# Batches 6 and 7 of a fused Mamba and mixture-of-experts kernel: two sums of the step size moved to VectorE, the gate products moved behind the scans of step 1

## The chip, the cores and the metric

The kernel runs on one core of one Trainium2 chip. The metric is the device time of one execution in microseconds (us); the number that counts is the median of several runs.

## The reference

The input `x` is 8 batches of 512 tokens with 128 features, float32. The result is `x + mamba(layernorm(x)) + moe(layernorm(x))`. What matters here is the Mamba block; per batch it computes:

```python
u = silu(causal_conv(xn @ in_proj))                   # 256 channels, 512 tokens
dt_raw, B, C = split(u @ x_proj)                      # 8, 16 and 16 columns
delta = softplus(dt_raw @ dt_proj.T + dt_proj_b)      # the step size
dA, dBu = exp(delta * A), delta * u * B               # for each of 16 states
h[t] = dA[t] * h[t-1] + dBu[t]                        # a scan along the tokens
y = sum over 16 states of h * C + u * D
y = y * silu(z)                                       # the gate
out = y @ out_proj + residual
```

The expert layer routes each token to 2 of 8 experts with 352 hidden units; its tiles of 128 tokens are worked off beside the scans of batches 1 to 5, and their results are gathered back in batches 5 to 7.

## The kernel before

The kernel is one program in which the order of the instructions of every engine is written out by hand; engines meet in counted semaphores, and each engine works through its own list in order. A wait that isn't met holds all that stands behind it on that engine.

The time is cut into 8 batches of 16 steps, one step for each state. Below, "step 6.3" is batch 6, state 3. The 256 channels lie as two halves of 128 partitions, so an ordinary operation is 128x512. In a step:

- ScalarE makes the decay factor `exp(delta * A)` of each half (`decay`, L502, into a buffer in SBUF; `decay_bank`, L514, into a bank of PSUM).
- The scan's input is either made by GpSimd (`scaled`, L915, in steps 6.0, 6.1, 6.2, 6.4, 7.0 and 7.1) or, in the other steps of batches 6 and 7 (the list `BY_PE`), by ScalarE in time-major form (`scaled`, L530, four instructions) and then transposed by TensorE into the scan's bank, one half at a time (`dbu_turn`, L1376).
- VectorE runs the scan of each half (`scan`, L1128), then multiplies each half with its row of C (`product`, L1145). In batches 6 and 7 both scans come before both products.
- TensorE transposes the products and adds them up over the states (`accumulate`, L1413). This happens in banks 2 and 3, a step later.

At the end of a batch ScalarE copies the sum out (`y_evac`, L681), TensorE turns it back to channel-major form in the same banks 2 and 3 (`y_turn`, L1506), and VectorE multiplies it with the gate (`gate`, L1153), which frees the banks for the next batch. So the first `accumulate` of a batch has a wait of its own:

```python
wait(pe, "p_rdy", 2 * (n + 1))
if k == 0:
    wait(pe, "g_rdy", 2 * b)
```

TensorE meets it in step 1. Behind it on TensorE stand, in step 6.1, `skip` (L1425), `rows(7)` (L1460) and a filler product `keep` (L1321); in step 6.2 the next `accumulate`, the first half of `dbu_turn` for step 6.3, a `skip` and a `keep`; and at the head of step 6.3 its second half. In step 7.1 the first half of `dbu_turn` for step 7.2 stands directly behind it, then a `keep`, then the second half.

Also at the start of batches 6 and 7 the scan's input in natural form is turned for ScalarE: TensorE writes it to banks 5 and 4 (`input_turn`, L1394), ScalarE copies it out (`input_turned`, L541). Bank 5 is the bank of the first scan of steps 6.1 and 7.1. In step 7.1 the scan waits for that copy itself:

```python
if b == NB - 1 and k == 1 and hf == 0:
    dve.wait_ge(s["dut_rdy"], 6)
```

The step size of the next batch is worked out beside the scans. In batch 6, for batch 7: ScalarE takes magnitudes (L740, L741) and `exp(-|v|)` (`vanishing`, L746) in steps 4 and 6, then in step 7 `rounded` (L751, `1 + y`, 128x1024) and `corrected` (L756, that minus 1), and the logarithm in step 10 (L761). GpSimd adds and corrects (`raise_sum`, L427; `correct`, L433) in steps 5 to 10. Right behind `corrected` ScalarE has the tanh of the z branch of batch 6 (`z_gate`, L664), VectorE follows with its product (L1244) at the end of step 6.8, and TensorE with the second z product (`z_mm`, L1498), which stands in front of the second half of `dbu_turn` for step 6.9.

GpSimd issues the indirect DMAs of the expert layer's gathers in these steps (L964).

Of the kernel before, what the change touches and what calls it, by code (L numbers as in the profile page):

```python
# [7 lines left out]
ALU = mybir.AluOpType  # L8
# [4 lines left out]
def build(nc, x, norm_w, w_in, conv_w, conv_b, x_proj, dt_proj, dt_b, a_log, d_par, w_out,  # L13
# [42 lines left out]
    with ctx:  # L56
        def sb(name, shape, dt=FP32):
            return ctx.enter_context(nc.sbuf_tensor(name, shape, dt))
# [81 lines left out]
        sp_y = sb("sp_y", [P, NH, T])  # L140
        sp_e = sb("sp_e", [P, NH, T])
        sp_d = sb("sp_d", [P, NH, T])
# [59 lines left out]
        s = {k: sem(k) for k in names}  # L202
# [57 lines left out]
        STEPS_AT = {b: (4, 6) if b == 6 else (2, 3) for b in range(NB - 1)}  # L260
        LOG_AT = {b: 10 if b == 6 else 8 for b in range(NB - 1)}
# [198 lines left out]
        def _(act):  # L460
# [179 lines left out]
            def late(b, k):  # L640

                if k in STEPS_AT[b]:
                    vanishing(b + 1, STEPS_AT[b].index(k))
                if k == STEPS_AT[b][1] + 1:
                    rounded(b + 1)
                if k == LOG_AT[b] - 3:
                    corrected(b + 1)
                if k == COLS_AT.get(b):
                    columns(b + 1)
# [356 lines left out]
        def _(dve):  # L1006
# [103 lines left out]
            def scan(b, k, hf):  # L1110

                n = b * S + k
                at = bank_of(b, 2 * k + hf)[:, :]
                dve.wait_ge(s["da_rdy"], 2 * n + hf + 1)
                if n in BY_PE:
                    dve.wait_ge(s["dbu_rdy"], 2 * turned_before(n) + hf + 1)
                    inp = at
                elif n == 0:
                    dve.wait_ge(s["dbu_0"], NH)
                    inp = dbu[0][:, hf, :]  # L1120
                else:
                    wait(dve, "dbu_p", 2 * pooled_before(n) + hf + 1)
                    inp = dbu[k % 2][:, hf, :]
                if b == NB - 1 and k == 1 and hf == 0:
                    dve.wait_ge(s["dut_rdy"], 6)
                elif b == NB - 1 and k == 1:
                    wait(dve, "p_rdy", 2 * S * b + 1)
                nc.vector.tensor_tensor_scan(at, da_of(n)[:, hf, :] if n in IN_SBUF else at, inp, 0.0,  # L1128
                                             ALU.mult, ALU.add).then_inc(s["h_rdy"], 1)
# [17 lines left out]
            def gate(b):  # L1147

                wait(dve, "o_mm", b)
                dve.wait_ge(s["yb_mm"], 2 * b + 2)  # L1150
                dve.wait_ge(s["z_rdy"], 2 * b + 2)
                for hf in range(NH):
                    nc.vector.tensor_tensor(g_sb[:, hf, :], zs_sb[:, hf, :], YB[hf][:, :], ALU.mult).then_inc(s["g_rdy"], 1)  # L1153
# [27 lines left out]
            def combine(b):  # L1181
# [4 lines left out]
                nc.vector.tensor_tensor(a_b, (GB, UB)[(b + 1) % 2][:, :].rearrange("p (t c) -> p t c", t=TT), a_b,  # L1186
                                        ALU.add).then_inc(s["comb"], 1)

            def step0(k):
                scan(0, k, 0)  # L1190
                scan(0, k, 1)
                product(0, k, 0)
                product(0, k, 1)
                if k in LATE_ROWS:
                    rows_normed(*LATE_ROWS[k])
                if k == 5:
                    st(nc.vector.reciprocal(irms[:, :], sxh))
                    st(nc.vector.tensor_tensor(irms[:, :], irms[:, :], rstd, ALU.mult))
                if k in (1, 4):
                    unit(1, k // 4)  # L1200
                if k == 7:
                    choices()
                if k in (11, 14):
                    unit(2, k // 14)
                if k in z_step(0):
                    z_gate(0, k)
                if k == 10:
                    weights()
                for g in HOT_STEP.get(k, ()):
                    one_hots(g)  # L1210

            def step(b, k):
                j = tile(b * S + k)
                scan(b, k, 0)
                if b >= 6:
                    scan(b, k, 1)
                if j is not None:
                    first_product(j)
                product(b, k, 0)
                if b < 6:  # L1220
                    scan(b, k, 1)
                if j is not None:
                    second_product(j)
                product(b, k, 1)
                if k == 0:
                    gate(b - 1)
                if b == 1 and k == 0:
                    sources()
                if b > 5 and k == PROJECT_AT[b] + 1:
                    store(b - 1, GB)  # L1230
                if b == 7 and k in z_step(b):
                    z_gate(b, k)
                elif b == 6 and k - 1 in z_step(b):
                    z_gate(b, k - 1)
                if k in (11, 14) and b + 2 < NB:
                    unit(b + 2, k // 14)
                if b * S + k in COMBINE_AT:
                    combine(COMBINE_AT[b * S + k])
# [62 lines left out]
            b = NB - 1  # L1301
# [480 lines left out]
```

## Time and profile before

| | |
|---|---|
| median of 3 runs | 633.02 us (633.02 to 634.33) |
| time of the profiled execution | 634.19 us |
| its span in the trace | 632.4 us |
| TensorE busy | 545.9 us (86%) |
| VectorE busy | 591.2 us (93%) |
| ScalarE busy | 457.4 us (72%) |
| GpSimd busy | 509.4 us (81%) |
| mean granted TensorE clock | 0.965 |

The profile gives one execution. PE is TensorE, DVE VectorE, ACT ScalarE, POOL GpSimd. The timeline view lists an engine's instructions in order of time, with like ones merged into one row (x2 for two); in square brackets stands how long the engine was idle before it, and what released it. The starts of the steps of batches 6 and 7 are read from the scans of VectorE: step 6.0 begins at 503.54 us, step 7.0 at 567.16 us.

### The profile page before, as it was taken

Reading aid. Unit: us, or ns where it says so; the run is one execution under the profiler, and the core shown is the slowest. Engines: PE = TensorE matmul, PEld = TensorE weight load, DVE = VectorE, ACT = ScalarE, POOL = GpSimd, SP = SyncE. Lnnn points to the kernel's source line nnn. Section 1 sums busy time; section 2 is a strip of 40 time slices with the busy share of each in tenths; the row PEclk is TensorE's granted clock in tenths of the full one; section 3 lists DMA queues with packets and bytes.
Section 4 is the critical chain, followed back from the end, with each engine's and each line's share of the span. In section 5 each row is a group of like instructions: output and inputs, shape, how many; then the busy total and the mean of one; then the engine's idle time right before and its main releaser. Section 6 shows DMA issues by size and latency. Waiting matters only on the chain.

```text
span 632.4 us, 11492 instructions
## 1 busy us (share of the span) xinstructions
PE 545.9 (86%) x3560; PEld 427.7 (68%) x3560; DVE 591.2 (93%) x852; ACT 457.4 (72%) x916; POOL 509.4 (81%) x481
## 2 busy tenths in 40 slices
PE   5969988888899998989899898998989697878887
PEld 2368765655877777777687677777777465656564
DVE  6967989999989998999989999899989999899997
ACT  1784899127877698667976688776986579969881
POOL 5795039638999989998999989999898978875783
PEclk9867979979999999999999999999999999899999
DMA  7320106834668788778878788678894345332473
GB/s 221 131 101 0 46 27 127 288 129 158 217 220 262 264 292 252 258 246 266 291 263 270 232 278 285 228 267 269 299 265 157 136 157 216 121 122 80 117 138 84
DMA packets 60894, 122.99 MB, mean 194 GB/s; under 512 B 8219, under 2 KB 41379, under 8 KB 53795
## 3 DMA queue, kind: packets, MB, share of 16 engines
q1 hardware_dynamic: 53826, 112.42, 52.3%
q0 software_dynamic: 6288, 9.52, 7.1%
q8 instruction: 29, 0.48, 0.3%
q10 hardware_dynamic: 720, 0.33, 0.3%
q14 instruction: 31, 0.25, 0.1%
HBM read 112.77 MB, written 9.47 MB: 193 GB/s over the span
## 4 chain that ended last, share of the span: by engine, by line
PE 43%; DVE 21%; ACT 18%; issue 15%; DMA 2%; POOL 0%; DVEq 0%; ACTq 0%
DVE bank L1128 8%; PE bank L1413 8%; PE bank L1562 7%; PE bank L1445 7%; DVE h_sb L1145 6%; PE bank L1576 5%; PE bank L1570 4%; ACT dbu L530 3%; ACT bank L514 2%; PE bank L1468 2%; ACT da L502 2%; PE bank L1460 2%; PE bank L1543 1%; PE bank L1376 1%; DVE lo_oh L1087 1%
## 5 line engine op out<-in xcount | busy, mean ns | idle before, releaser
L915 POOL TENSOR_TENSOR dbu<-du,xn_all 128x512 f32<-128x512 f32 x172 | 215.4, 1275 | 26.8 <-DVE bank L1128 26.4
L1128 DVE TENSOR_TENSOR_SCAN bank<-bank,dbu 128x512 f32<-128x512 f32 x170 | 207.2, 1221 | 9.0 <-ACT bank L514 8.9
L1145 DVE TENSOR_TENSOR h_sb<-bank,xh_all 128x512 f32<-128x512 f32 x240 | 159.3, 678 | 1.2
L514 ACT ACTIVATE bank<-delta,a_sb 128x512 f32<-128x512 f32 x170 | 116.8, 689 | 54.2 <-DVE h_sb L1145 53.5
L1413 PE MATMUL bank<-id_sb,h_sb 128*128 128x128 f32 x992 | 134.8, 281 | 15.2 <-DVE h_sb L1145 13.6
L1413 PEld LDWEIGHTS bank<-id_sb,h_sb 128*128 128x128 f32 x992 | 115.3, 145 | 26.8 <-DVE h_sb L1145 20.4
L1128 DVE TENSOR_TENSOR_SCAN bank<-da,bank 128x512 f32<-128x512 f32 x82 | 96.7, 1214 | 17.1 <-PE bank L1376 17.0
L1562 PEld LDWEIGHTS bank<-wd_sb,hid 117*128 117x128 f32 (+1 forms) x432 | 55.1, 190 | 57.8 <-DVE hid L1179 33.1
L1562 PE MATMUL bank<-wd_sb,hid 117*128 117x128 f32 (+1 forms) x432 | 63.7, 283 | 28.3 <-ACT xT L687 26.7
L902 POOL DMA_INDIRECT xs<-xn_rows,src x72 | 70.7, 981 | 12.4 <-issue 9.1
L530 ACT ACTIVATE dbu<-du_t,bc_sb 128x256 f32<-128x256 f32 x164 | 69.4, 496 | 4.5 <-DVE bank L1128 2.9
L1376 PE MATMUL bank<-id_sb,dbu 128*128 128x128 f32 x328 | 54.2, 291 | 18.2 <-ACT dbu L530 10.1
L1376 PEld LDWEIGHTS bank<-id_sb,dbu 128*128 128x128 f32 x328 | 39.8, 148 | 40.2 <-issue 22.2
L1445 PE MATMUL bank<-xhT,wk_sb 128*128 128x512 f32 x128 | 61.3, 607 | 0.7 <-ACT xhT L473 0.7
L502 ACT ACTIVATE da<-delta,a_sb 128x512 f32<-128x512 f32 x86 | 58.0, 713 | 4.7 <-DVE bank L1128 4.5
L1570 PE MATMUL bank<-xT,wgu_sb 128*118 128x128 f32 x432 | 59.2, 273 | 0.3 <-DVE ga L1172 0.2
L1576 PE MATMUL bank<-xT,wgu_sb 128*118 128x128 f32 x432 | 59.1, 272 | 0.0
L964 POOL DMA_INDIRECT xhT<-y_slots,slot x40 | 38.7, 966 | 18.5 <-DVE bank L1128 6.8
L1576 PEld LDWEIGHTS bank<-xT,wgu_sb 128*118 128x118 f32 x432 | 52.7, 181 | 0.5 <-issue 0.5
L1570 PEld LDWEIGHTS bank<-xT,wgu_sb 128*118 128x118 f32 x432 | 52.3, 182 | 0.7 <-issue 0.7
L705 ACT ACTIVATE ys<-bank,stat 128x128 f32<-128x128 f32 x72 | 26.3, 366 | 33.1 <-PE bank L1562 33.0
L698 ACT ACTIVATE th<-bank 118x384 f32<-118x384 f32 x72 | 34.8, 483 | 19.1 <-PE bank L1570 18.4
(197 smaller groups left out, 902.9 us busy)
## 6 DMA issues: line engine op xcount, KB each, us to landing
xh_all<-b_rows SPq DMA_DIRECT2D x30, 1024.0 KB, 7.2
xn_all<-b_rows SPq DMA_DIRECT2D x25, 1024.0 KB, 7.2
wgu_sb<-in_w_gu SPq DMA_DIRECT2D x72, 352.0 KB, 2.9
wd_sb<-in_w_dn SPq DMA_DIRECT2D x72, 192.0 KB, 3.3
y_slots<-ys SPq DMA_DIRECT2D x72, 64.0 KB
xn_rows<-xn_all SPq DMA_DIRECT2D x2, 1040.0 KB, 9.9
out<-x_sb SPq DMA_DIRECT2D x7, 256.0 KB, 6.8
x_sb<-in_x SPq DMA_DIRECT2D x2, 640.0 KB, 5.7
```

The lines of the kernel that those rows point to most:

```text
L514: nc.scalar.activation(bank_of(b, m)[:, :], delta[b % 2][:, hf, :], ACT.Exp, scale=a_sb[:, hf, k:k + 1]).then_inc(s["da_rdy"], 1)
L530: last = nc.scalar.activation(dbuT[k % 2][:, t, :], duT[:, t, :], ACT.Copy, scale=bc_sb[q][:, t, k:k + 1])
L902: nc.gpsimd.indirect_dma_start(xs[i][:, :], None, xn_rows, bass.IndirectOffsetOnAxis(ap=src[:, j:j + 1], axis=0)).then_inc(s[f"xs_in{i}"], 16)
L915: nc.gpsimd.tensor_tensor(dbu[k % 2][:, hf, :], du[b % 2][:, hf, :], b_ring[c % 2][:, k % CH, :], ALU.mult).then_inc(s["dbu_p"], 1)
L1128: nc.vector.tensor_tensor_scan(at, da_of(n)[:, hf, :] if n in IN_SBUF else at, inp, 0.0, ALU.mult, ALU.add).then_inc(s["h_rdy"], 1)
L1145: nc.vector.tensor_tensor(h_sb[k % 2][:, hf, :], bank_of(b, 2 * k + hf)[:, :], row, ALU.mult).then_inc(s["p_rdy"], 1)
L1376: last = nc.tensor.transpose(at[:, t * P:(t + 1) * P], dbuT[k % 2][:, t, hf * P:(hf + 1) * P], id_sb[:, :])
L1413: last = MM(HT[i][:, t % 2, hf * P:(hf + 1) * P], h_sb[k % 2][:, hf, t * P:(t + 1) * P], id_sb[:, :], is_transpose=True, start=(k == 0 and ...
L1445: last = MM(at[:, :], wk_sb[:, tap, hf * P:(hf + 1) * P], xhT[:, c, tap:tap + T], start=(tap == taps[0] if c == 0 else tap == 0), stop=(ta ...
L1562: last = MM(XD[:, P:P + H], hid[j % 2][0:FN[c], c * P:(c + 1) * P], wd_sb[j % NW][0:FN[c], c, :], start=(c == 0), stop=(c == NF - 1))
L1570: last = MM(GB[0:FW, c * P:(c + 1) * P], wgu_sb[j % NW][:, c * FS:c * FS + FW], xT[j % 2][:, :], start=True, stop=True)
L1576: last = MM(UB[0:FW, c * P:(c + 1) * P], wgu_sb[j % NW][:, F + c * FS:F + c * FS + FW], xT[j % 2][:, :], start=True, stop=True)
```

## The change

Two things. In batch 6 `rounded(7)` and `corrected(7)` leave ScalarE (both in step 6.7) and are done by VectorE as `tensor_scalar` instructions of 128x1024, the first at the end of step 6.7, the second at the end of step 6.8, each behind the step's products and ahead of the z product. In batches 6 and 7 the two gate products of the batch before leave the end of step 0; they now stand in step 1, behind both scans and ahead of both products. Batches 1 to 5 stay as they are. The waits of the other engines are unchanged.

```diff
@@ ScalarE, late(b, k)
-                if k == STEPS_AT[b][1] + 1:
+                if b < 6 and k == STEPS_AT[b][1] + 1:
                     rounded(b + 1)
-                if k == LOG_AT[b] - 3:
+                if b < 6 and k == LOG_AT[b] - 3:
                     corrected(b + 1)
@@ VectorE
+            def rounded(c):
+
+                dve.wait_ge(s["sp_exp"], 2 * c + 2)
+                nc.vector.tensor_scalar(sp_d[:, :, :], sp_y[:, :, :], 1.0, None, ALU.add).then_inc(s["sp_w"], 1)
+
+            def corrected(c):
+
+                dve.wait_ge(s["sp_w"], c)
+                nc.vector.tensor_scalar(sp_e[:, :, :], sp_d[:, :, :], -1.0, None, ALU.add).then_inc(s["sp_corr"], 1)
+
@@ VectorE, step(b, k)
                 scan(b, k, 0)
                 if b >= 6:
                     scan(b, k, 1)
+                if b >= 6 and k == 1:
+                    gate(b - 1)
                 if j is not None:
                     first_product(j)
                 product(b, k, 0)
@@ VectorE, step(b, k)
                 product(b, k, 1)
-                if k == 0:
+                if b < 6 and k == 0:
                     gate(b - 1)
+                if b == 6 and k == STEPS_AT[b][1] + 1:
+                    rounded(b + 1)
+                if b == 6 and k == STEPS_AT[b][1] + 2:
+                    corrected(b + 1)
```

## Rows read from the trace of the kernel before

**Rows 1.** The page, part 1: busy us, share of the span, instructions.

```profile
PE 545.9 (86%) x3560; PEld 427.7 (68%) x3560; DVE 591.2 (93%) x852; ACT 457.4 (72%) x916; POOL 509.4 (81%) x481
```

**Rows 2.** Windows view: stretch, its us, busy by engine, granted PE clock, DMA, GB/s.

```profile
519.40:529.60 10.20, 8.41 (x55) 6.28 (x54) 10.20 (x13) 10.20 (x22) 8.10 (x9) 1.00 0.64 246
575.80:625.00 49.20, 44.21 (x274) 31.36 (x272) 49.20 (x60) 38.04 (x79) 35.17 (x27) 1.00 0.50 113
...
568.00:570.00 2.00, 2.00 (x12) 2.00 (x11) 2.00 (x4) 2.00 (x5) 1.84 (x3) 0.52 0.97 401
```

**Rows 3.** Timeline, VectorE, steps 6.0 to 6.3: start, duration, instruction, [idle before, releaser].

```profile
507.57 1.28 DVE L1153 TENSOR_TENSOR g_sb<-zs_sb,bank 128x512 f32<-128x512 f32 x2 [0.52 <-issue]
508.77 2.34 DVE L1128 TENSOR_TENSOR_SCAN bank<-bank,dbu 128x512 f32<-128x512 f32 x2
...
512.21 2.48 DVE L1128 TENSOR_TENSOR_SCAN bank<-bank,dbu 128x512 f32<-128x512 f32 x2
...
515.78 2.48 DVE L1128 TENSOR_TENSOR_SCAN bank<-da,bank 128x512 f32<-128x512 f32 x2
```

**Rows 4.** Timeline, TensorE, steps 6.0 to 6.3; seven merged rows left out.

```profile
507.27 1.62 PE L1321 MATMUL bank<-wk_sb,id_sb 128*128 128x512 f32 x2
509.00 1.07 PE L1413 MATMUL bank<-id_sb,h_sb 128*128 128x128 f32 x8
...
516.33 0.60 PE L1376 MATMUL bank<-id_sb,dbu 128*128 128x128 f32 x4
```

**Rows 5.** Timeline, ScalarE: decay factors of step 6.1 and the first of 6.2.

```profile
506.30 1.94 ACT L514 ACTIVATE bank<-delta,a_sb 128x512 f32<-128x512 f32 x3
```

**Rows 6.** Timeline, GpSimd: the inputs of step 6.1; a gather in step 6.7.

```profile
504.51 2.50 POOL L915 TENSOR_TENSOR dbu<-du,xn_all 128x512 f32<-128x512 f32 x2
...
533.10 0.94 POOL L964 DMA_INDIRECT xhT<-y_slots,slot  x1 [0.30 <-DVE h_sb L1145]
```

**Rows 7.** Timeline, ScalarE, step 6.7: the two sums and the tanh behind them.

```profile
535.35 1.14 ACT L751 ACTIVATE sp_d<-sp_y,sign_sb 128x1024 f32<-128x1024 f32 x1
536.52 1.15 ACT L756 ACTIVATE sp_e<-sp_d,sign_sb 128x1024 f32<-128x1024 f32 x1
537.58 0.58 ACT L664 ACTIVATE zs_sb<-bank 128x512 f32<-128x512 f32 x1
```

**Rows 8.** Timeline, VectorE: scans of 6.8, z product, second scan of 6.9.

```profile
533.33 2.33 DVE L1128 TENSOR_TENSOR_SCAN bank<-da,bank 128x512 f32<-128x512 f32 x2
...
538.26 0.69 DVE L1244 SCALAR_TENSOR_TENSOR zs_sb<-zs_sb,bank 128x512 f32<-128x512 f32 x1 [1.43 <-ACT zs_sb L664]
...
541.90 1.23 DVE L1128 TENSOR_TENSOR_SCAN bank<-da,bank 128x512 f32<-128x512 f32 x1 [1.81 <-PE bank L1376]
```

**Rows 9.** Timeline, TensorE: z product, then second half of the turn for 6.9.

```profile
539.00 1.93 PE L1498 MATMUL bank<-xhT,wz_sb 128*128 128x512 f32 x2 [4.01 <-DVE zs_sb L1244]
540.73 1.06 PE L1376 MATMUL bank<-id_sb,dbu 128*128 128x128 f32 x4
```

**Rows 10.** One line of code: count, min/median/max ns, first and last start, forms.

```profile
L1255 DVE TENSOR_SCALAR sp_d<-sp_y x2: 411/414/417, 26.5 to 28.2; 128x512 f32<-128x512 f32 x2
L827 POOL TENSOR_SCALAR xn_all<-x_sb,mean,both x32: 786/836/2047, 10.5 to 46.5; 128x128 f32<-128x128 f32 x32
```

**Rows 11.** Timeline, VectorE: gate products in step 7.0, scans of step 7.2.

```profile
571.17 1.29 DVE L1153 TENSOR_TENSOR g_sb<-zs_sb,bank 128x512 f32<-128x512 f32 x2 [0.51 <-issue]
...
575.81 2.33 DVE L1128 TENSOR_TENSOR_SCAN bank<-da,bank 128x512 f32<-128x512 f32 x2
```

**Rows 12.** Timeline, ScalarE: the copy of the turned input in step 7.0.

```profile
570.73 1.07 ACT L541 ACTIVATE du_t<-bank 128x512 f32<-128x512 f32 x2
```

**Rows 13.** Timeline, TensorE: accumulate of 6.15 and 7.0, first turn for 7.2.

```profile
566.69 1.97 PE L1413 MATMUL bank<-id_sb,h_sb 128*128 128x128 f32 x8 [2.89 <-DVE h_sb L1145]
...
572.61 1.07 PE L1413 MATMUL bank<-id_sb,h_sb 128*128 128x128 f32 x8 [1.53 <-DVE g_sb L1153]
574.66 0.66 PE L1376 MATMUL bank<-id_sb,dbu 128*128 128x128 f32 x4 [0.99 <-ACT dbu L530]
```

## The prediction, made before the changed kernel ran

> **What bounds the kernel now.** I read the page's busy shares first: VectorE is the busiest engine, 591.2 us of a span of 632.4, TensorE follows with 545.9 [rows 1]. The share alone says little about an edit in two places of batch 6 and one of batch 7, so the windows come next. From 575.80 to 625.00 VectorE is busy for 49.20 of 49.20 us: whatever is lost or won before step 7.2 stays to the end, as nothing later can absorb it. From 519.40 to 529.60 VectorE and ScalarE are both full [rows 2]. Then the timelines of the places touched, engine by engine. The reader is to look for the brackets: VectorE stands idle for 0.52 us ahead of the gate in step 6.0 [rows 3], for 0.51 us in step 7.0 [rows 11], for 1.43 us ahead of the z product and for 1.81 us ahead of the second scan of step 6.9 [rows 8]. These are the only places where the change can win. The other question is who waits for the gate.
>
> The pace of an undisturbed step on VectorE is 508.77 to 512.21, so 3.44 us, of which the two products take 1.19 us and the scans 2.24 us; two gate products move the next start by 508.77 - 507.57 = 1.20 us [rows 3]. From the end of an instruction to the start of what it releases I take 0.15 us into TensorE (gate ends at 508.85, `accumulate` starts at 509.00 [rows 3, 4]), 0.10 us into VectorE (tanh ends at 538.16, product starts at 538.26 [rows 7, 8]) and 0.11 us from TensorE into VectorE (541.79, 541.90 [rows 8, 9]).
>
> **The gate in batch 6.** VectorE is free at 507.05 (507.57 - 0.52). With the gate gone from there it starts the scans of step 6.1, if their operands are ready: ScalarE's first decay factor of three ends near 507.0 (506.30, three in 1.94 us [rows 5]), GpSimd's second input half at 507.01 [rows 6]. So 507.10, 1.67 us earlier than 508.77. The gate follows at 507.10 + 2.24 = 509.34 and ends at 510.62; before, it ended at 508.85. The step is over at 507.10 + 3.44 + 1.20 = 511.74 instead of 512.21. That is the gain, 0.47 us, and on VectorE alone it would stay.
>
> But the first `accumulate` of the batch waits for the gate, and TensorE is in order. It started at 509.00, as soon as the gate was done; behind it stand nine merged rows without a gap, the last of them the second half of `dbu_turn` for step 6.3, which ends at 516.93 [rows 4]. The scan that needs it already waited for it: the pair of step 6.3 takes 2.48 us where an undisturbed one takes 2.34 or 2.33 [rows 3, 8]. So this chain of 7.93 us was the bound at step 6.3 before, by a hair. Now it starts at 510.62 + 0.15 = 510.77, **1.77 us later**, and ends at 518.70; the second scan of step 6.3 starts at 518.81 instead of 517.04. VectorE, early by 0.5 us at step 6.2, stands idle in step 6.3 and leaves it 1.77 us late. The next decay factors of ScalarE and everything on TensorE are released from there, so all engines move together: +1.77 us. The bounds: TensorE is idle from 508.89 to 510.77, 1.88 us. It kept its full clock after 1.53 us idle and was at half after 2.89 us [rows 13]. I take the full clock. At half for as long as it was after 566.69 (566.69 to about 569.9, where the window shows 0.52, the 1.2 GHz level [rows 2, 13]) the chain would be about 1.6 us longer, so +3.4 us; not below +1.77, unless the wait doesn't bind (rivals).
>
> **The two sums.** ScalarE loses 537.58 - 535.35 = 2.23 us in step 6.7 [rows 7]. It was full there [rows 2], and its tanh released the z product of VectorE after 1.43 us of idle time. The new tanh ends at 538.16 + 1.77 - 2.23 = 537.70. What is late next is VectorE itself, since both sums now stand ahead of the z product. Its price: the same instruction on 128x512 takes 414 ns [rows 10]; twice the elements cost between that and 828 ns, and I take 0.65 us each, because part of the 414 ns is fixed and neighbours overlap by a few hundredths. Step 6.8 starts at 533.33 + 1.77 + 0.65 = 535.75, its products end 3.43 later, `corrected` takes 0.65, and the z product starts at 539.83 instead of 538.26: +1.57. So a stall of 1.50 us (538.26 against 533.33 + 3.43) is replaced by 1.30 us of work. The gain is **0.20 us**, between 0.67 (0.41 each) and -0.16 (0.83 each). The wait of 1.81 us behind it stays: TensorE's z product starts when VectorE's ends, after 4.01 us idle before and about 3.8 us now, at half clock (two products in 1.93 us), then the turn [rows 9]. At the full clock these two would take about half and VectorE would gain some 1.1 us (its own first scan covers the rest); I don't expect that. `rounded` needs the exponentials of step 6.6, which come before it on ScalarE by the order of the steps, and the logarithm of step 6.10 finds its operand. GpSimd's `correct` stands in step 6.9. The rest of batch 6 is at VectorE's pace, +1.57 us.
>
> **The sums against GpSimd.** The rows show that two engines can be in each other's way here: GpSimd's 128x128 `tensor_scalar` took 836 ns at the median and up to 2047 while VectorE ran instructions of this kind, and VectorE's own stayed at 411 to 417 ns [rows 10]. So I add nothing for VectorE, and up to 0.94 us each, one gather [rows 6], as the upper bound. The Trainium skill (SBUF — State Buffer, section "SBUF: two separate sides") says that a VectorE instruction in a 2-port mode and a GpSimd instruction share one port pair as an exclusive lock, and that whichever starts first keeps it for its whole length. By that rule VectorE could lose; it is rival 2 below, priced from rows.
>
> **The gate in batch 7.** Times here are those of before; the 1.57 us come on top. VectorE is free at 571.17 - 0.51 = 570.66 [rows 11]. It cannot start step 7.1 then: its first scan waits for the copy of the turned input, which ScalarE ends at 571.80 [rows 12]. Before, the gate covered that wait; its cover is gone. So scans from 571.90, gate from 574.14 to 575.43, products, free at 576.54: 0.73 us later than 575.81 already. And again `accumulate` waits for the gate: 575.43 + 0.15 = 575.58 instead of 572.61. TensorE is idle since 571.08 (572.61 - 1.53), 4.5 us, more than the 2.89 and 4.01 us after which it was found at half clock [rows 9, 13]. So `accumulate` costs 1.97 us (its successor starts some 0.2 us before its modelled end), the first half of the turn for step 7.2 costs 1.06 us [rows 9, 13]: 575.58 + 1.77 + 1.06 + 0.11 = 578.52 for the first scan of step 7.2, instead of 575.81. **+2.71 us.** At the full clock: 0.90 + 0.63 instead of 1.77 + 1.06, so 577.2 and +1.4 us. The lower bound is the +0.73 of VectorE's own list.
>
> **Sum.** +1.77 - 0.20 + 2.71 = +4.28 us. The profiled execution had a span of 632.4 us and a time of 634.19 us, 1.17 us over the median; I put the sum on the median: 633.02 + 4.28 = 637.3 us. A profile of the new kernel should have a span near 636.7 us.
>
> **The rivals.**
> 1. TensorE is at its full clock in step 7.1: 1.57 + 1.4 = +3.0 us, 636.0 us. For it speaks that it had been busy until 571.08; against it the two rows after shorter or like idle times.
> 2. VectorE's two sums are held up by GpSimd. Relative to step 6.8 the first would meet the gather of 533.10 to 534.04 at 533.33 [rows 6] and lose 0.71 us, the second likewise some 0.3 us: 4.28 + 1.0 = +5.3 us, 638.3 us. Against it: VectorE's 411 to 417 ns beside a busy GpSimd [rows 10].
> 3. TensorE is at half clock behind the gate of step 6.1 too: +5.9 us, 638.9 us.
> 4. The other side: the gate isn't what TensorE waits for, because it would be held up there anyhow. Then the chain at step 6.3 doesn't move. Batch 6 gives -0.8 us (-0.6 at step 6.3, and 1.30 us of sums for 1.50 of stall), batch 7 +0.73 us: -0.1 us, 632.9 us. It decides from the point at which the chain ends before 516.93. Where in addition ScalarE's copy in step 7.0 came early enough (before 570.6), step 7.2 would start at 570.66 + 4.64 = 575.30, -0.51 us, and the kernel would be faster: -1.3 us, 631.7 us. Against both: TensorE starts 0.15 us after the gate in batch 6, the bracket of 572.61 names the gate as its releaser [rows 3, 4, 13], and the copy has a row.
> 5. The change does what it says for ScalarE, but it wins nothing since the z product goes behind `corrected`; that is in the sum.
>
> **How the numbers follow.** Forecast 0.45, rival 1 0.17, rival 2 0.15, rival 3 0.06, rival 4 0.11 at 632.9 and 0.06 at 631.7. The predicted time is the likeliest, 637.3 us. The range reaches from 634.6 (rival 1 with a z product at the full clock and cheap sums is 634.5) to 639.4 (rival 3 with dear sums), and leaves out rival 4 and little else. A measurement of this kernel tells about 0.2%, 1.3 us, from no change: faster 0.06, same 0.11, slower 0.83.
>
> **What would show it.** Right: in step 6.1 scans from about 507.1, gate behind them; TensorE's `accumulate` released by the gate at 510.8; VectorE idle ahead of both scans of step 6.3; no idle time ahead of the z product, but some 1.8 us ahead of the second scan of 6.9; VectorE idle 1.2 us ahead of 7.1 and about 2 us ahead of 7.2; a granted clock near 0.5 around 577 to 580. Wrong: step 6.3 starting at 515.2; the two sums at more than 0.9 us; the clock at 1.00 in step 7.1. If the step from 6.4 to 7.0 is shorter than before by more than 0.7 us, my account of the sums is wrong.

## The result, and the profile after

The changed kernel takes 638.19 us at the median of 6 runs (637.41 to 639.50), the kernel before 633.02 us (630.77 to 634.33, 6 runs): a ratio of 1.0085, 95% interval 1.0060 to 1.0111. It is 5.2 us slower. The span of the profiled execution is 637.7 us, 5.3 us over the 632.4 us of before. The forecast was 637.3 us.

The starts of VectorE's scans, read from the timelines, say where it went:

| stretch | before, us | changed, us | difference | forecast |
|---|---|---|---|---|
| start to step 6.0 | 503.54 | 503.48 | -0.06 | 0 |
| step 6.0 to 6.4 | 15.82 | 17.53 | +1.71 | +1.77 |
| step 6.4 to the z product in 6.8 | 18.90 | 18.60 | -0.30 | -0.20 |
| z product to step 6.11 | 9.98 | 10.66 | +0.68 | 0 |
| step 6.11 to 7.0 | 18.92 | 18.91 | 0 | 0 |
| step 7.0 to 7.3 | 12.07 | 15.36 | +3.29 | +2.71 |
| step 7.3 to the end | 53.17 | 53.16 | 0 | 0 |

**Step 6.0 to 6.4.** VectorE's timeline (start, duration, instruction, in brackets the idle time and what ended it), against [rows 3]:

```profile
506.99 2.35 DVE L1128 TENSOR_TENSOR_SCAN bank<-bank,dbu 128x512 f32<-128x512 f32 x2
509.24 1.26 DVE L1153 TENSOR_TENSOR g_sb<-zs_sb,bank 128x512 f32<-128x512 f32 x2
...
511.62 2.34 DVE L1128 TENSOR_TENSOR_SCAN bank<-bank,dbu 128x512 f32<-128x512 f32 x2
...
516.93 1.23 DVE L1128 TENSOR_TENSOR_SCAN bank<-da,bank 128x512 f32<-128x512 f32 x1 [1.80 <-PE bank L1392]
518.69 1.23 DVE L1128 TENSOR_TENSOR_SCAN bank<-da,bank 128x512 f32<-128x512 f32 x1 [0.53 <-PE bank L1392]
```

The scans of step 6.1 start at 506.99 instead of 508.77, the gate follows at 509.24, step 6.2 is 0.6 us early. Then VectorE stands idle for 1.80 and 0.53 us ahead of the scans of step 6.3. The same on TensorE, against [rows 4]:

```profile
510.65 1.07 PE L1429 MATMUL bank<-id_sb,h_sb 128*128 128x128 f32 x8 [1.82 <-DVE g_sb L1153]
...
517.98 0.60 PE L1392 MATMUL bank<-id_sb,dbu 128*128 128x128 f32 x4
```

Its `accumulate` is released by the gate, after 1.82 us idle; the second half of the turn for step 6.3 ends at 518.58, 7.93 us after that start, the same length as before (509.00 to 516.93).

**The two sums and the z product**, VectorE, against [rows 8]:

```profile
534.98 0.68 DVE L1192 TENSOR_SCALAR sp_d<-sp_y 128x1024 f32<-128x1024 f32 x1
...
539.01 0.68 DVE L1197 TENSOR_SCALAR sp_e<-sp_d 128x1024 f32<-128x1024 f32 x1
539.61 0.68 DVE L1260 SCALAR_TENSOR_TENSOR zs_sb<-zs_sb,bank 128x512 f32<-128x512 f32 x1
...
543.37 1.23 DVE L1128 TENSOR_TENSOR_SCAN bank<-da,bank 128x512 f32<-128x512 f32 x1 [1.95 <-PE bank L1392]
...
545.93 1.23 DVE L1128 TENSOR_TENSOR_SCAN bank<-da,bank 128x512 f32<-128x512 f32 x1 [0.15 <-PE bank L1392]
547.36 1.23 DVE L1128 TENSOR_TENSOR_SCAN bank<-da,bank 128x512 f32<-128x512 f32 x1 [0.20 <-PE bank L1392]
```

Each sum takes 0.68 us, 0.60 from start to start. No idle time is left ahead of the z product; the one ahead of the second scan of step 6.9 is there still (1.95 instead of 1.81 us), and two new ones follow in step 6.10 (0.15 and 0.20 us). TensorE shows why, against [rows 9]:

```profile
540.34 2.07 PE L1514 MATMUL bank<-xhT,wz_sb 128*128 128x512 f32 x2 [3.69 <-DVE zs_sb L1260]
542.21 1.06 PE L1392 MATMUL bank<-id_sb,dbu 128*128 128x128 f32 x4
543.06 1.92 PE L1429 MATMUL bank<-id_sb,h_sb 128*128 128x128 f32 x8
```

It starts the z product at half clock as before, but stays there longer. The windows of the changed kernel (stretch, its us, busy of PE, PEld, DVE, ACT, POOL, the granted clock, DMA share, GB/s):

```profile
542.00:544.00 2.00, 2.00 (x10) 1.79 (x9) 0.63 (x1) 0.70 (x2) 1.68 (x3) 0.50 0.25 80
544.00:546.00 2.00, 2.00 (x10) 1.96 (x9) 1.84 (x4) 2.00 (x5) 1.82 (x2) 0.51 0.14 37
```

and of the kernel before in the same stretch:

```profile
542.00:544.00 2.00, 2.00 (x14) 1.73 (x13) 2.00 (x3) 2.00 (x5) 1.72 (x2) 0.85 0.13 37
544.00:546.00 2.00, 2.00 (x17) 1.74 (x16) 2.00 (x3) 1.98 (x4) 1.81 (x2) 1.00 0.19 57
```

0.50 and 0.51 (1.2 GHz) against 0.85 and 1.00. GpSimd's gathers in the two places where the sums run:

```profile
534.74 1.05 POOL L964 DMA_INDIRECT xhT<-y_slots,slot  x1 [0.30 <-DVE h_sb L1145]
...
538.51 1.30 POOL L964 DMA_INDIRECT xhT<-y_slots,slot  x1 [0.30 <-DVE h_sb L1145]
```

Both were under way when a sum began on VectorE (534.98, 539.01). Both sums took the same 0.68 us; the gathers took 1.05 and 1.30 us instead of 0.94.

**Step 7.0 to 7.3**, VectorE, against [rows 11]:

```profile
573.95 2.35 DVE L1128 TENSOR_TENSOR_SCAN bank<-da,dbu 128x512 f32<-128x512 f32 x2 [1.26 <-ACT du_t L541]
576.21 1.26 DVE L1153 TENSOR_TENSOR g_sb<-zs_sb,bank 128x512 f32<-128x512 f32 x2
...
580.52 1.23 DVE L1128 TENSOR_TENSOR_SCAN bank<-da,bank 128x512 f32<-128x512 f32 x1 [1.85 <-PE bank L1392]
582.22 1.23 DVE L1128 TENSOR_TENSOR_SCAN bank<-da,bank 128x512 f32<-128x512 f32 x1 [0.48 <-PE bank L1392]
```

1.26 us of idle time ahead of step 7.1, ended by ScalarE's copy; then 1.85 and 0.48 us ahead of the two scans of step 7.2. TensorE, against [rows 13]:

```profile
577.62 1.94 PE L1429 MATMUL bank<-id_sb,h_sb 128*128 128x128 f32 x8 [4.09 <-DVE g_sb L1153]
579.35 1.06 PE L1392 MATMUL bank<-id_sb,dbu 128*128 128x128 f32 x4
580.20 1.06 PE L1337 MATMUL bank<-wk_sb,id_sb 128*128 128x256 f32 x2
581.06 1.06 PE L1392 MATMUL bank<-id_sb,dbu 128*128 128x128 f32 x4
```

`accumulate` is released by the gate after 4.09 us idle and takes 1.94 us; the turns take 1.06 us each, both of them, and the filler between them too.

### The profile page after: what moved, and what is told of

It reads as the page before. It is cut to its first block, busy times and chain, and to the rows that moved or that the text cites. A ratio compares the mean times of both kernels' runs of the same rounds, so it can differ in the third digit from the quotient of the medians.

```text
span 637.7 us, 11492 instructions
## 1 busy us (share of the span) xinstructions
PE 548.4 (86%) x3560; PEld 431.0 (68%) x3560; DVE 592.5 (93%) x854; ACT 455.2 (71%) x914; POOL 509.9 (80%) x481
## 4 chain that ended last, share of the span: by engine, by line
PE 45%; DVE 20%; ACT 17%; issue 15%; POOL 1%; DMA 1%; DVEq 0%; ACTq 0%; POOLq 0%
PE bank L1429 8%; DVE bank L1128 7%; PE bank L1578 7%; PE bank L1461 6%; DVE h_sb L1145 6%; PE bank L1592 5%; PE bank L1586 5%; ACT bank L514 2%; PE bank L1484 2%; PE bank L1392 2%; ACT dbu L530 2%; PE bank L1476 2%; ACT da L502 2%; PE bank L1559 1%; DVE lo_oh L1087 1%
## 5 line engine op out<-in xcount | busy, mean ns | idle before, releaser
L1392 PEld LDWEIGHTS bank<-id_sb,dbu 128*128 128x128 f32 x328 | 41.2, 152 | 37.6 <-issue 22.5
```

Source lines behind the costliest of these rows:

```text
L1392: last = nc.tensor.transpose(at[:, t * P:(t + 1) * P], dbuT[k % 2][:, t, hf * P:(hf + 1) * P], id_sb[:, :])
```

## The experiments

The theory: the loss is made by what stands behind the gate's wait on TensorE, and in step 7.1 also by TensorE's clock and by ScalarE's copy. The rivals: the sums on VectorE cost it; or only VectorE's own list counts. The experiments ran in three groups, each group's kernels on one chip with its own runs of the kernel before: 636.85, 635.75 and 635.85 us at their medians, where the first runs had 633.02. Ratios are against these runs. A ratio of a few tenths of a per cent with an interval as wide says little, so the stretches of the traces carry the argument.

**One part alone.** First the sums without the gate's move:

```diff
-                if b >= 6 and k == 1:
-                    gate(b - 1)
-                if b < 6 and k == 0:
+                if k == 0:
                     gate(b - 1)
```

> Only the two sums of the step size go to VectorE (steps 6.7 and 6.8, ahead of the z product); the gate products stay in step 0 of every batch. Theory (the gate's wait on TensorE makes the loss): step 6.3 undisturbed as before; the z product starts 0.3 us earlier than before (a stall of 1.50 us becomes 1.20 us of work), step 6.10 moves by -0.3 us, or up to +0.3 us if TensorE stays longer at its lower clock behind the z product; span within 0.5 us of the 632.4 us of before. Rival (the sums on VectorE cost it, by themselves or through GpSimd's gathers): a good part of the 5.3 us is here, a span of 634 us or more, with instructions of the sums over 0.9 us each or VectorE idle in front of them.

Measured: ratio 1.0016 (0.9988 to 1.0044), span 633.8 us. The span missed the bound of the theory by 0.9 us and nearly reached the 634 us of the rival. VectorE had idle time ahead of step 6.8 (1.37 us) and ahead of the second scan of step 7.6 (2.18 us) that neither of the first two traces had. (The expectations call this second place step 7.9; counted by VectorE's scans it is step 7.6.) So this trace can't be set beside the first one in those stretches. One more thing in it matters below. No edit of this kernel touches step 6.0, yet TensorE's turn of y ran at its full clock there:

```profile
502.45 1.09 PE L1520 MATMUL bank<-id_sb,g_sb 128*128 128x128 f32 x8 [0.74 <-ACT g_sb L681]
```

The gate then waited for nothing, and step 6.0 to 6.4 took 15.20 us instead of 15.82.

The other two parts, with the sums back on ScalarE in both:

```diff
# gate of batch 5 alone (batch 6 the same with b == 7 and b < 7)
-                if b >= 6 and k == 1:
+                if b == 6 and k == 1:
                     gate(b - 1)
-                if b < 6 and k == 0:
+                if b != 6 and k == 0:
                     gate(b - 1)
```

> Only the gate products of batch 5 move, from the end of step 6.0 to behind the scans of step 6.1; the sums stay on ScalarE, batch 7 as before. Theory: TensorE's first accumulate is released by the gate 1.7 us later, VectorE stands idle ahead of both scans of step 6.3, whose second starts 1.7 us late; ScalarE's tanh is late by the same, and all to the end: +1.7 us, up to +2.3 us if TensorE is longer at its lower clock after the z product; a span of 634.1 to 634.7 us. Rival (VectorE's earlier start of step 6.1 is a gain that stays, the loss is made elsewhere): step 6.4 starts 0.4 us early, a span near 632.0 us.

Measured: ratio 1.0047 (1.0011 to 1.0084), span 635.0 us, 0.3 us over the expectation. VectorE's timeline:

```profile
514.07 1.23 DVE L1128 TENSOR_TENSOR_SCAN bank<-da,bank 128x512 f32<-128x512 f32 x1 [1.79 <-PE bank L1388]
515.84 1.23 DVE L1128 TENSOR_TENSOR_SCAN bank<-da,bank 128x512 f32<-128x512 f32 x1 [0.53 <-PE bank L1388]
```

The same two idle times ahead of step 6.3 as in the changed kernel, and step 6.0 to 6.4 takes 17.53 us, to the hundredth the same.

> Only the gate products of batch 6 move, from the end of step 7.0 to behind the scans of step 7.1; all else as before. Theory: VectorE idle 1.2 us ahead of step 7.1 (ScalarE's copy), TensorE released 3 us later and at half clock, VectorE idle 1.9 us ahead of step 7.2 and again ahead of its second scan; step 7.3 starts 2.7 to 3.3 us late; a span of 635.1 to 635.7 us. Rival (only VectorE's own list counts, that is the wait for the copy): +0.7 us, 633.1 us.

Measured: ratio 1.0035 (1.0006 to 1.0064), span 638.4 us, 2.7 us over the upper expectation, with idle times of 1.95 us ahead of step 6.8 and 2.17 us in step 7.6. VectorE:

```profile
572.56 2.35 DVE L1128 TENSOR_TENSOR_SCAN bank<-da,dbu 128x512 f32<-128x512 f32 x2 [1.27 <-ACT du_t L541]
...
579.12 1.23 DVE L1128 TENSOR_TENSOR_SCAN bank<-da,bank 128x512 f32<-128x512 f32 x1 [1.84 <-PE bank L1388]
580.55 1.23 DVE L1128 TENSOR_TENSOR_SCAN bank<-da,bank 128x512 f32<-128x512 f32 x1 [0.20 <-PE bank L1388]
```

Step 7.0 to 7.3 takes 15.10 us, within the 14.8 to 15.4 that was expected over the 12.07 of before. The rival's 12.8 is out. But the two other kernels of this group so far, whose gate stays in step 7.0, need 12.63 and 12.78 us for the stretch, so within the group the move costs 2.3 to 2.5 us.

**The same two kernels once more**, since the idle times needed a cause:

> The kernel before once more, unchanged, for a trace from the chip of this group: the first group's four traces have idle times of VectorE ahead of steps 6.8 (1.4 to 2.0 us) and 7.9 (2.2 us) that neither of the first two traces had. Theory (a matter of the execution, not of the edits): if this chip shows them, they stand in this trace too, and its step 6.4 to 7.0 takes about 48.5 us instead of 47.8; rival (they come from the edits): none here, 47.8 us.

Measured: 637.11 us, span 635.3 us. VectorE has them here too:

```profile
533.64 1.23 DVE L1128 TENSOR_TENSOR_SCAN bank<-da,bank 128x512 f32<-128x512 f32 x1 [2.17 <-PE bank L1376]
...
576.41 2.59 DVE L1128 TENSOR_TENSOR_SCAN bank<-da,bank 128x512 f32<-128x512 f32 x2
...
592.98 2.34 DVE L1128 TENSOR_TENSOR_SCAN bank<-da,bank 128x512 f32<-128x512 f32 x2 [1.93 <-remote]
```

and step 6.4 to 7.0 takes 49.92 us, more than the 48.5 expected. So these idle times don't come from any edit. All that the scan of step 6.8 waits for had been done (in the trace of the third kernel the turn ends at 533.56, the scan starts at 535.33); what held it isn't shown. Only the kernels before and changed of the very first traces were without them. What the sums alone cost stays open: step 6.4 to 7.0 takes 50.01 us with them on VectorE and 49.92 in this repeat without, but 48.70 and 48.48 in the two kernels of the first group that have them on ScalarE.

The repeat shows a second thing. Step 7.0 to 7.3 takes 12.75 us in it, not 12.07, with no edit at all: TensorE is at half clock in the turn for step 7.2, VectorE is idle for 0.92 us ahead of the gate instead of 0.51, and the pair of scans of step 7.2 takes 2.59 us (second line above) instead of 2.33.

```profile
576.61 1.06 PE L1376 MATMUL bank<-id_sb,dbu 128*128 128x128 f32 x4
```

> The changed kernel once more, for a second trace of it, from the chip of this group: how far do the stretches repeat? Theory: step 6.0 to 6.4 takes 17.5 us again (it hangs on a chain of instructions with fixed lengths), step 7.0 to 7.3 between 14.7 and 15.4 us (TensorE's lower clock begins and ends there, which may fall otherwise). Rival (the differences between two traces are as large as the effect): 6.0 to 6.4 or 7.0 to 7.3 off by more than 1 us.

Measured: 640.94 us, span 639.1 us. Step 6.0 to 6.4 takes 17.53 us and step 7.0 to 7.3 15.34 us (15.36 in the first trace). In the changed kernel the two stretches of the effect repeat to some hundredths; step 6.4 to 7.0, at 50.02 us instead of 48.17, doesn't. Repeat against repeat, the change costs 17.53 - 15.83 = 1.70 us, 50.02 - 49.92 = 0.10 us and 15.34 - 12.75 = 2.59 us, together 4.4 us.

**The clock.** Fillers in the idle time of step 7.0:

```diff
                 if k == 0:
                     y_turn(b - 1)
+                if b == NB - 1 and k == 0:
+                    pe.wait_ge(s["hid_rdy"], NJ)
+                    pe.wait_ge(s["comb"], 1)
+                    for i in range(4):
+                        keep(UB[:, :])
```

> The whole change, and in step 7.0 TensorE has four more filler products of 512 columns behind the turn of y, in the time in which it stands idle until the gate; they use nothing that others need. Theory, its part on the clock: the fillers keep the granted clock at 1.00 until the gate is done, so accumulate takes 1.1 us and the turn 0.6 us; the first scan of step 7.2 starts 1.2 us earlier than in the changed kernel and its second scan isn't held up a second time: span 1.2 to 1.9 us below the changed kernel's 637.7, at 635.8 to 636.5 us; 1.4 us of loss at step 7.2 stay, for the place in the queue alone. Rival (TensorE's clock doesn't matter, the wait alone does): 637.7 us as the changed kernel.

Measured: ratio 1.0058 (1.0018 to 1.0098), span 637.6 us, not below the changed kernel's first trace, with idle times in steps 6.8 and 7.6 again; but step 7.0 to 7.3 takes 13.49 us instead of 15.36, 1.87 us less. TensorE and VectorE:

```profile
572.60 3.60 PE L1337 MATMUL bank<-wk_sb,id_sb 128*128 128x512 f32 x8
577.15 1.06 PE L1429 MATMUL bank<-id_sb,h_sb 128*128 128x128 f32 x8 [0.96 <-DVE g_sb L1153]
578.05 0.60 PE L1392 MATMUL bank<-id_sb,dbu 128*128 128x128 f32 x4
```

```profile
578.76 2.34 DVE L1128 TENSOR_TENSOR_SCAN bank<-da,bank 128x512 f32<-128x512 f32 x2 [0.55 <-PE bank L1392]
```

`accumulate` takes 1.06 us and the turn 0.60, as in a stretch at the full clock, and the second scan isn't held up a second time. 0.55 us of idle time ahead of step 7.2 stay, for the place in the queue.

**The place in the queue.** TensorE's other work goes ahead of the wait, and the two fillers that stood behind it, in steps 6.1 and 7.1, are dropped:

```diff
+                if b == 6 and k == 1:
+                    rows(7)
+                if b == 7 and k == 1:
+                    dbu_turn(b, 2, (0,))
+                    pe.wait_ge(s["hid_rdy"], NJ)
+                    pe.wait_ge(s["comb"], 1)
+                    keep(UB[:, :])
                 if k > 0:
                     accumulate(g - 1)
-                if g + 1 in BY_PE:
+                if g + 1 in BY_PE and not (b == 7 and k == 1):
                     dbu_turn(b, k + 1, (0,))
...
-                    if k == ROWS_AT[b]:
+                    if b < 6 and k == ROWS_AT[b]:
                         rows(b + 1)
...
-                if b == 5 and k >= 12 or b == 6 and k < 7:
+                if b == 5 and k >= 12 or b == 6 and k < 7 and k != 1:
...
-                elif b == 7 and k in (1, 3, 5, 12):
+                elif b == 7 and k in (3, 5, 12):
```

> The whole change, but TensorE does other work ahead of its wait for the gate: rows(7) in step 6.1, and in step 7.1 the first half of the turn for step 7.2 and one wide filler; the filler products that stood behind the wait in steps 6.1 and 7.1 are gone. Theory (the loss is what stands behind the gate's wait in TensorE's queue): no idle time ahead of step 6.3, and step 6.0 to 6.4 takes 15.0 us (17.53 in the changed kernel, 15.82 before); step 7.0 to 7.3 takes 12.8 us, up to 13.7 if TensorE is at its lower clock there (15.36 changed, 12.07 before), the 0.7 us over before being VectorE's wait for ScalarE's copy. Rival (the scans wait for something else that comes late with the gate): both stretches stay within 0.5 us of the changed kernel's.

Measured: ratio 1.0021 (1.0001 to 1.0041), span 636.4 us. In batch 6 the theory's number came: 15.00 us from step 6.0 to 6.4, no idle time ahead of step 6.3. In batch 7 it was a miss: 15.27 us. TensorE and VectorE:

```profile
574.19 1.11 PE L1392 MATMUL bank<-id_sb,dbu 128*128 128x128 f32 x4 [3.74 <-ACT dbu L530]
575.10 1.91 PE L1337 MATMUL bank<-wk_sb,id_sb 128*128 128x512 f32 x2
576.80 1.91 PE L1429 MATMUL bank<-id_sb,h_sb 128*128 128x128 f32 x8
578.51 1.01 PE L1392 MATMUL bank<-id_sb,dbu 128*128 128x128 f32 x4
```

```profile
576.09 1.22 DVE L1128 TENSOR_TENSOR_SCAN bank<-da,bank 128x512 f32<-128x512 f32 x1
579.63 1.23 DVE L1128 TENSOR_TENSOR_SCAN bank<-da,bank 128x512 f32<-128x512 f32 x1 [2.31 <-PE bank L1392]
```

The first half of the turn was in time and step 7.2 started without idle time. But TensorE had been idle for 3.74 us and was at half clock, so that the wide filler in front of the wait took 1.91 us and kept `accumulate` until 576.80, where the gate was done at 574.98; the second scan stood idle for 2.31 us. The filler that was to cure the clock was too late for it and stood in the way. So the next kernel has the four fillers of step 7.0 and the turn ahead of the wait, without that filler:

```diff
                 if b == 7 and k == 1:
                     dbu_turn(b, 2, (0,))
-                    pe.wait_ge(s["hid_rdy"], NJ)
-                    pe.wait_ge(s["comb"], 1)
-                    keep(UB[:, :])
...
+                if b == NB - 1 and k == 0:
+                    pe.wait_ge(s["hid_rdy"], NJ)
+                    pe.wait_ge(s["comb"], 1)
+                    for i in range(4):
+                        keep(UB[:, :])
```

> The whole change, with both cures in step 7: four fillers behind the turn of y in step 7.0, as in the kernel with fillers, and the first half of the turn for step 7.2 ahead of the wait for the gate, as in the kernel with TensorE's work first, but no filler between them and the wait; step 6.1 with rows(7) first and no filler. Theory (the loss in batch 7 is the sum of three things: 0.7 us for ScalarE's copy, 0.7 us for the place in TensorE's queue, the rest for its clock): step 7.0 to 7.3 takes 12.8 us and VectorE is idle there only ahead of step 7.1. Rival (there is a further cause): 13.5 us or more. Step 6.0 to 6.4 takes 15.0 us as with the work first.

Measured: ratio 1.0002 (0.9982 to 1.0022), span 634.3 us. Step 6.0 to 6.4 takes 14.99 us, step 7.0 to 7.3 12.84 us, and VectorE is idle there only for the 1.26 us ahead of step 7.1. TensorE:

```profile
574.04 0.66 PE L1392 MATMUL bank<-id_sb,dbu 128*128 128x128 f32 x4 [0.21 <-ACT dbu L530]
574.98 1.07 PE L1429 MATMUL bank<-id_sb,h_sb 128*128 128x128 f32 x8 [0.28 <-DVE g_sb L1153]
```

With TensorE's list cured, the two stretches take 27.83 us together, against 27.89 in the first trace of before and 28.58 in its repeat; VectorE's list is exactly that of the changed kernel. The cure is of several parts (order, four fillers more, two fewer), and no kernel has the new order with the old fillers. The runs agree, on another chip: the interval ends at 1.0022, that of the changed kernel begins at 1.0060.

**Can the idle times be used otherwise?** The sums behind the z product, the gate in step 0 as before:

```diff
-                if b == 6 and k == STEPS_AT[b][1] + 1:
-                    rounded(b + 1)
-                if b == 6 and k == STEPS_AT[b][1] + 2:
-                    corrected(b + 1)
...
                 elif b == 6 and k - 1 in z_step(b):
                     z_gate(b, k - 1)
+                    if k == 8:
+                        rounded(b + 1)
+                        corrected(b + 1)
```

> The gate products in step 0 as before; both sums on VectorE, but at the end of step 6.8 behind the z product instead of ahead of it. Theory: ScalarE's tanh comes 2.2 us earlier, the z product starts at once behind step 6.8's products (1.5 us earlier than before), and the two sums of 1.2 us run while TensorE makes its z product and the turn for step 6.9, in what was 1.81 us of idle time: the second scan of step 6.9 starts 1.4 us earlier than before relative to step 6.7, or 0.6 us less than that if TensorE stays longer at its lower clock; about -1.4 us in all. Rival (the 1.2 us of the sums are paid in full wherever they stand): no more than 0.3 us won.

Measured: ratio 1.0008 (0.9990 to 1.0026), span 634.7 us. The second scan of step 6.9 starts 7.30 us after step 6.8, against 8.57 in the first trace of before: the gain of 1.3 us is there where the z product used to wait for ScalarE. But with the idle time ahead of step 6.8, which all traces of this group have, ScalarE isn't late: there the kernel with the gate of batch 6 alone moved, its sums on ScalarE, needs 7.20 us for the same. 0.65 us are left against the repeat of before in the stretch from step 6.7 to the second scan of 6.9 (13.20 against 13.85), and nothing against the kernel with the gate of batch 6 alone moved (12.96); neither theory is confirmed by its number.

Then fillers in steps 5.13 to 5.15, 6.8 and 6.15:

```diff
+                if b == 5 and k >= 13:
+                    pe.wait_ge(s["ga_rdy"], NJ)
+                    keep(GB[:, :])
+                if b == 6 and k in (8, 15):
+                    pe.wait_ge(s["hid_rdy"], NJ)
+                    wait(pe, "comb", k // 15)
+                    for i in range(2 + k // 15):
+                        keep(UB[:, :])
```

> As the kernel with the sums behind the z product, and TensorE gets wide filler products in idle times: one more in each of steps 5.13 to 5.15, two in 6.8, three in 6.15. Theory (the lower clock behind an idle TensorE prolongs what VectorE waits for): the turn of y in steps 6.0 and 7.0 runs at the full clock and the gates start without their 0.5 us of idle time; the z product and the turn for 6.9 take 1.7 us instead of 2.8, so that the second scan of step 6.9 waits for nothing; in all 2.5 to 3.3 us less than before, 0.4 to 0.5%. Rival (the clock is not what these waits hang on): the same time as the kernel with the sums behind z.

Measured: ratio 0.9987 (0.9965 to 1.0008), span 632.7 us against 635.3 of before in this group. TensorE:

```profile
503.68 1.09 PE L1519 MATMUL bank<-id_sb,g_sb 128*128 128x128 f32 x8 [0.74 <-ACT g_sb L681]
```

```profile
537.32 1.91 PE L1511 MATMUL bank<-xhT,wz_sb 128*128 128x512 f32 x2 [3.04 <-DVE h_sb L1145]
```

In step 6.0 the turn of y takes 1.09 us, not 1.97, the gate waits for nothing, and step 6.0 to 6.4 takes 15.21 us instead of 15.83. The kernel with the sums alone on VectorE had the same without these fillers (1.09 and 15.20 us), so one trace doesn't show that they did it. Step 7.0 to 7.3 takes 11.74 us instead of 12.76. In step 6.8 nothing is won: after 3.04 us idle the z product runs at half clock. The spans differ by 2.6 us, the runs by less than they can tell.

The last kernel has three fillers instead of two in step 6.8 and none in step 6.1:

```diff
-                    for i in range(2 + k // 15):
+                    for i in range(3):
...
-                if b == 5 and k >= 12 or b == 6 and k < 7:
+                if b == 5 and k >= 12 or b == 6 and k < 7 and k != 1:
```

> The kernel with the sums behind z and fillers, with three fillers instead of two in step 6.8 and without the one of step 6.1. Theory: TensorE keeps its full clock into the z product (2.0 us there instead of 2.8 with the turn behind it) and the second scan of step 6.9 waits for nothing, 0.7 us gained, if TensorE is idle less than 2.2 us in front of it; step 6.3 starts without its 0.15 us: 1 us below that kernel, 3 to 3.5 us below the kernel before in the same group. Rival (the clock falls all the same, or the filler comes in the way): no gain over two fillers.

Measured: ratio 1.0003 (0.9981 to 1.0025), span 631.6 us. TensorE:

```profile
535.84 2.07 PE L1511 MATMUL bank<-xhT,wz_sb 128*128 128x512 f32 x2 [2.80 <-DVE zs_sb L1257]
```

2.80 us idle even behind three fillers, half clock again: the gain in step 6.9 didn't come. Step 6.3 lost its 0.15 us (15.06 from 6.0 to 6.4). The turn of y in step 6.0 takes 1.09 us here too. The fillers of step 6.15, ahead of step 7.0, are the same in both kernels, but the 11.74 us didn't come back: step 7.0 to 7.3 takes 12.78 us, with TensorE at half clock (1.06 us for the turn) and VectorE idle again ahead of both scans of step 7.2:

```profile
574.56 1.23 DVE L1128 TENSOR_TENSOR_SCAN bank<-da,bank 128x512 f32<-128x512 f32 x1 [0.48 <-PE bank L1389]
```

The low span of 631.6 us isn't a gain of the edit: step 6.0 began at 499.76 us, while in kernels with no edit ahead of it that start lies anywhere from 500.48 to 503.54. No kernel here is shown to beat the one before.

## Why the prediction was right

- **The gate in batch 6**: right in mechanism and size. +1.71 us for +1.77 (+1.70 in the repeats); the gate alone gives the same 17.53 us, and TensorE's work ahead of the wait gives 15.00. That TensorE would be at its full clock there held too: the chain had its length of 7.93 us.
- **The two sums**: 0.60 us each instead of 0.65, so -0.30 us up to the z product instead of -0.20. That VectorE's own two sums stand in place of its wait for ScalarE held in the first pair of traces. It rests on that wait of 1.43 us. In the three later traces with the sums on ScalarE VectorE is idle ahead of step 6.8 instead and no longer waits for ScalarE behind it, so there the account isn't confirmed.
- **Against GpSimd**: VectorE lost nothing, rival 2 is out. The rule of the Trainium skill (SBUF — State Buffer, section "SBUF: two separate sides"), by which the one that starts first keeps the port pair for its whole length, isn't what the rows show if a gather is taken as holding the pair from its start to its end: it had begun first both times, and it was the one that got longer, by 0.11 and 0.36 us. Which ports the two instructions used, and when, no run shows.
- **Behind the z product**: off, and not by the change. I took the wait of 1.81 us as unchanged and nothing behind it; from the z product the second scan of 6.9 is 0.12 us later, step 6.10 another 0.24 and 6.11 another 0.32 us, together 0.68, because TensorE was at 0.50 and 0.51 where before it had 0.85 and 1.00. Why the clock rose later is open. From the z product to step 6.11 the unchanged kernel took 9.98 us in one trace and 10.66 in the other, the changed one 10.66 and 10.11: this term goes with the execution, and the zero of the forecast isn't shown to be wrong for the change.
- **The gate in batch 7**: right in mechanism, low in size against the first trace: +3.29 for +2.71 (repeat against repeat +2.59). VectorE's idle time for ScalarE's copy (1.26 us) and ahead of the first scan (1.85 us for 1.98) were as forecast. What the sum lacks is the second half of the turn for step 7.2: it prices the first half at half clock and stops there, at nothing for the filler and the second half; both ran at half clock too, and VectorE stood idle for another 0.48 us. The fillers show that this is the clock: 1.87 us of the 3.29 go with them, and TensorE is at its full clock there in both kernels that have them. The turn ahead of the wait takes another 0.65 us (13.49 to 12.84). What stays over the first trace of before, 0.77 us, is VectorE's own list: the cover that the gate gave the copy, forecast at 0.73. Against the repeat of before it is 0.09 us, because there VectorE is idle longer ahead of the gate (0.92 us) and waits for the turn.
- **The clock in batch 7 came partly by luck.** I read it off the idle time just ahead of the work: full after 1.53 us, half after 2.89. The runs don't bear that out as a rule. The turn of y in step 6.0 stood behind 0.74 us of idle time in all 13 traces and ran at half clock in ten of them. And in the repeat of before TensorE was at half clock in step 7.1 (0.50 from 574.90 to 578.20) behind idle times of only 1.53 and 0.57 us. So half clock was right for the changed kernel, but a part of its price is paid by the kernel before too, in some executions.
- **Rivals 1, 3 and 4**: TensorE was at half clock in step 7.1 and not in 6.1; and the gate was what it waited for.

The sum came to 4.28 us and the measured difference is 5.2 to 5.3 us. The 1.0 us between is TensorE's clock in two places, 0.68 us behind the z product and 0.58 us in batch 7, less small terms; the two traces of the unchanged kernel differ by 0.68 us in either stretch. In the repeats the three stretches give 4.4 us.

## What to carry to other kernels

When work is moved later on one engine to hide its wait, look at who waits for its result and at the whole queue behind that waiter: here 0.5 us of VectorE's idle time was removed, and the engine that fed VectorE was held 1.8 and 3 us longer. Work in an engine's list that needs nothing from the moved result can be put ahead of the wait; that, with the engine kept busy ahead of it and two fillers behind it dropped, gave the loss back. A filler helps only where it keeps the engine busy in time: four of them right behind the last work in step 7.0 gave 1.87 us back, one directly in front of the wait in step 7.1 ran at half clock and held `accumulate` for 1.7 us, and two or three in step 6.8 left 3.04 and 2.80 us of idle time and won nothing. And before a difference is laid to an edit, trace the unchanged kernel twice: here one stretch of it took 12.07 and 12.75 us.

## What the runs showed of the hardware

Where a `tensor_scalar` of VectorE (128x1024) ran beside a gather that GpSimd had begun, the gather took 1.05 and 1.30 us instead of 0.94, while VectorE's instruction kept its 0.68 us. In the later traces with the sums on VectorE the gathers beside them took 1.02 to 1.15 us, but for one at 0.94 that a sum met only in its last 0.1 us; the sums took 0.68 to 0.76 us. TensorE was found at half clock after 4.09, 3.74, 3.04, 2.80 us idle, and at its full clock after 1.82; after 2.88 us (568.72 in the changed kernel) it began at the full clock and was at half from 570; after 0.74 us (the turn of y in step 6.0) it was at half in ten traces and at full in three. So the idle time just ahead doesn't decide it by itself. How long it then stayed at half differed between two executions of nearly the same work (about 3 us and over 5 us behind the z product). VectorE had idle times of 1.4 to 2.3 us ahead of step 6.8, and up to 2.2 us in step 7.6, in all traces but the first two, that of the unchanged kernel among them; in the trace of the third kernel what the scan of step 6.8 waits for had been done before, and the cause is open. The spans of the unchanged kernel, 632.4 and 635.3 us, differ by 2.9 us. That is why the verdicts above rest on stretches and not on whole times.
